# A transformer and cluster block on one core: layer norm with its roots in PSUM, an earlier start of attention, and setup loads moved beside other stages

## The chip, the cores and the metric

One core of a Trainium2 chip (trn2) runs the whole program. The metric is the device time of one execution in microseconds (us); less is better. Engines are named as in the profile: PE (TensorE, the matrix engine), DVE (VectorE), ACT (ScalarE), POOL (GpSimd) and SP (SyncE, which only issues DMAs here).

## The reference, cut to what matters

The input x has the shape 2 x 96 x 256 x 256, float32. Two layers follow each other, each added to its input.

```python
# layer 0
g   = group_norm(x, 32 groups)                 # statistics over 3 channels and all pixels
tok = overlapping 16x16 windows of g, step 14  # 19 x 19 windows per image
y   = layer_norm over the 96 channels of tok
q, k, v = y@wq, y@wk, y@wv                     # 4 heads, 16 wide for q and k, 24 for v
tok = softmax(q k^T / 4) v @ wproj + tok       # windows added up, shared strips halved
x2  = tok put back on the map
h   = gelu(layer_norm(x2) @ fc1 + b)
h   = h + gelu(depthwise_conv_5x5(h) + b)
x   = x + (h @ fc2 + b + x2)
# layer 1
x   = x + cluster(group_norm(x))               # similarity to 4 centres per region, per head
```

## The kernel before

`program` (line 2099) runs eight stages in a row. Each stage is a block: five instruction streams, one for each engine, joined by semaphores, and the next block starts when all of them have ended.

**group_norm_statistics** (line 49). SP loads x in 16 tiles of 3 MB (128 partitions x 24 KB) into a ring of four buffers, DVE takes `bn_stats` of each (line 102) and at the end one `bn_aggr` for each image (line 107). Beside it POOL and ACT lay out the taps of the convolution and store them (lines 85 and 95); ACT issues those DMAs.

**attention_setup** (line 111). POOL clears four small tables, SP issues 15 small loads of weights and constants (lines 144 to 153), and then a chain of small linked operations on DVE, PE and ACT makes the scale and shift of the group norm for each channel and image, and folds the weights of the layer norm into wq, wk and wv. The shift of q and k by the layer norm's bias is kept as a 97th row of `wqk` (lines 199 and 201).

**layer_norm** (line 217). The map is laid out as 128 partitions = four row blocks (2 images x 2 halves) of 32 channels, with three channel groups in the free dimension. There are 16 tiles of 8 rows, and each is cut into four chunks of 512 pixels: 64 chunks. 24 tiny DMAs (line 270) first copy scale and shift into this layout, and one more (line 271) loads the matrix of ones. A tile is moved by 12 DMAs of 256 KB in (line 278) and 12 out (line 286), all issued by SP, in six buffers and four tiles ahead. For each chunk ACT applies scale and shift (line 334, three instructions), PE sums over channels with the ones (line 309), DVE subtracts the mean, which it reads in PSUM (line 354), POOL squares (line 298), PE sums the squares (line 317), DVE copies the variance from PSUM to SBUF (line 358). When a tile's four variances are there, ACT makes 1/sqrt by Ln and Exp over the whole tile in SBUF (lines 339 and 341), and DVE multiplies (line 350), two tiles behind the subtraction. The order on DVE and ACT is written out by `slots`. The result goes to `y_attention` in HBM.

**attention** (line 371). The map is cut into 38 bands of 16 rows (19 per image) with 19 windows each. SP loads a band of y in two halves (`load_y`, line 496), POOL turns its eight pieces to column order (line 582), PE makes queries and keys of a piece (line 705, 512 columns) in the one bank `lin_ps`, ACT copies them to `packed` (line 655), and SP spreads a pair of pieces by eight DMAs to the heads' rows of q and k (`spread_heads`, line 522). Then each window takes one step: scores for the maximum on PE (line 720), maxima on DVE (801), turned maxima (766) added to q (842), scores (732), Exp on ACT (668), values (750), products (743), normalisation on POOL (590 to 611). At the start of the first band POOL clears two tables and q, DVE writes a row of ones into y and fills k, and PE and ACT wait for all six of these fills. All eight pieces are projected and spread before the first window's scores, which wait for all four pairs. For later bands the pieces are placed in the steps of the band before (`qk_at`).

**fc1**, **conv**, **fc2** (line 1308). fc2 works through 14 tiles; SP and ACT issue its loads and stores. Its block ends when all stores have landed (lines 1392 and 1468).

**cluster_setup** (line 1504). SP issues 18 small loads (line 1562). DVE reduces the sums that fc2 left (1624), PE gathers them once all 18 loads are there (1586), and a chain follows like that of attention_setup: among it 64 linked tiny operations (lines 1669 and 1670), then 16 for `rhs` (1675, 1676) and four copies (1679).

**cluster** (line 1682) follows and is not touched.

The order in the layer norm before is set by these lines:

```python
for k in range(AHEAD):
    load(k)
for k in range(NT):
    sp.wait_ge(z_done, (k + 1) * PER)
    ...
    if k + AHEAD < NT:
        load(k + AHEAD)
```

## Time and profile before

| | before |
|---|---|
| median of 3 runs | 6937.62 us (6933.67 to 6956.9) |
| the profiled execution: its own time | 6937.03 us |
| its span, first to last instruction | 6935.3 us |
| mean granted TensorE clock | 0.943 of full |
| PE busy | 6015.5 us (87% of the span) |
| DVE busy | 5209.9 us (75%) |
| ACT busy | 3497.3 us (50%) |
| POOL busy | 2286.0 us (33%) |
| DMA | 1252.65 MB, mean 181 GB/s |

The busy shares are means over stages with different limits. PE is at work nearly all the time in attention, whose steps the diff leaves as they are; the diff is about the stretches before 700 us and around 6050 us, where the shares of all engines are low or differ. So the reading goes by stretches and by the order of time in them, not by the table.

### The profile page before, as it was taken

The numbers are of one execution on the slowest core, as the hardware profiler recorded it, in microseconds if no ns is written. First come the engines' busy times: TensorE is split into PE (matmuls) and PEld (weight loads), VectorE is DVE, ScalarE is ACT, GpSimd is POOL, SyncE is SP. The second block draws the span as 40 slices with busy tenths as digits, with TensorE's granted clock in tenths as the row PEclk, the third lists the DMA queues.
The fourth block names the chain that finished last, engine by engine and source line by source line (L and its number), as shares of the span: only waits on it lengthen the run. The fifth ranks groups of instructions, "written<-read, shape, count | busy, mean of one in ns | idle before, by whom it ended". The sixth has DMA issues, their size and how long they took to land. (4 is left out here: it accounts for less than half of the span.)

```text
span 6935.3 us, 135783 instructions
## 1 busy us (share of the span) xinstructions
PE 6015.5 (87%) x51768; PEld 3118.6 (45%) x51768; DVE 5209.9 (75%) x7712; ACT 3497.3 (50%) x5182; POOL 2286.0 (33%) x4080
## 2 busy tenths in 40 slices
PE   0885999999999999999999689989998666578887
PEld 0332555555555555555555233335555111066663
DVE  7686888888888888888888455558887445456666
ACT  0553666666666666666666356644443111144431
POOL 0343455555554555555554656610000000000000
PEclk9997999999999999999999799999999788789987
DMA  7786344444444444444443598888987999835667
GB/s 306 192 240 179 72 106 101 101 104 106 103 108 100 103 109 102 105 101 101 107 96 71 146 269 235 237 288 345 345 341 266 283 314 316 249 90 167 189 183 248
DMA packets 761666, 1252.65 MB, mean 181 GB/s; under 512 B 159364, under 2 KB 477828, under 8 KB 730948
## 3 DMA queue, kind: packets, MB, share of 16 engines
q1 hardware_dynamic: 700532, 1090.77, 55.8%
q10 hardware_dynamic: 54560, 111.50, 5.3%
q0 software_dynamic: 5936, 41.68, 1.7%
q8 instruction: 422, 6.91, 0.4%
q14 instruction: 216, 1.77, 0.1%
HBM read 680.81 MB, written 508.40 MB: 171 GB/s over the span
## 5 line engine op out<-in xcount | busy, mean ns | idle before, releaser
L801 DVE TENSOR_REDUCE at_mz<-at_ps 128x4 bf16<-128x1024 f32 x1444 | 1772.3, 1227 | 105.3 <-PE at_ps L720 80.3
L668 ACT ACTIVATE at_E<-at_ps 128x1024 f32<-128x1024 f32 x1444 | 1399.4, 1021 | 382.6 <-PE at_ps L732 368.0
L732 PE MATMUL at_ps<-at_qaug,at_k 32*128 32x256 f32 x11552 | 830.0, 401 | 23.7 <-DVE at_qaug L842 23.7
L743 PE MATMUL at_ps<-at_E,at_vaug 128*32 128x256 f32 x11552 | 774.3, 385 | 5.5
L1282 PE MATMUL cv_ps<-cv_yin,cv_band 128*128 128x384 f32 x2304 | 745.4, 486 | 26.2 <-DMA cv_yin<-y_mlp 26.2
L1302 DVE TENSOR_TENSOR cv_yin<-cv_gl,cv_yin 64x384 f32<-64x384 f32 x1152 | 637.6, 553 | 150.3 <-ACT cv_gl L1293 142.4
L732 PEld LDWEIGHTS at_ps<-at_qaug,at_k 32*128 32x128 f32 x11552 | 523.0, 184 | 494.1 <-issue 384.5
L590 POOL TENSOR_TENSOR at_share<-at_rden,t_share 128x8 f32<-128x8 f32 x722 | 148.5, 206 | 1445.5 <-DVE at_rden L812 1445.5
L1282 PEld LDWEIGHTS cv_ps<-cv_yin,cv_band 128*128 128x128 f32 x2304 | 436.1, 189 | 335.7 <-DMA cv_yin<-y_mlp 27.1
L720 PE MATMUL at_ps<-at_k,at_q 32*128 32x256 bf16 x5776 | 574.2, 275 | 8.9 <-DMA at_k<-at_packed 7.4
L1293 ACT ACTIVATE cv_gl<-cv_ps,cv_bias 128x384 f32<-128x384 f32 x576 | 335.1, 582 | 435.8 <-PE cv_ps L1282 435.8
L842 DVE TENSOR_TENSOR at_qaug<-at_ps,at_q 128x256 f32<-128x256 f32 x722 | 306.5, 425 | 272.3 <-PE at_ps L766 272.3
L750 PEld LDWEIGHTS at_ps<-t_wv,at_y 96*128 96x128 f32 x2888 | 377.1, 190 | 297.6 <-issue 297.6
L750 PE MATMUL at_ps<-t_wv,at_y 96*128 96x96 f32 x2888 | 495.5, 294 | 0.0
L1566 POOL MEMSET cs_eps<- 96x1 f32 x1 | 0.1, 96 | 1502.8 <-POOLq L1314 1502.8
L676 ACT ACTIVATE at_xa<-at_ps,t_out_shift 96x448 f32<-96x448 f32 (+2 forms) x304 | 314.7, 1035 | 347.4 <-PE at_ps L759 347.4
L1432 DVE SCALAR_TENSOR_TENSOR f_xa<-f_ps,f_b,f_xa 128x256 f32<-128x256 f32 x384 | 226.9, 666 | 348.4 <-PE f_ps L1415 347.5
L1859 PE MATMUL cl_ps<-c_rhs,cl_xu 97*128 97x208 f32 x2048 | 448.0, 376 | 41.1 <-DMA cl_xu<-x 34.6
L1859 PEld LDWEIGHTS cl_ps<-c_rhs,cl_xu 97*128 97x128 f32 x2048 | 397.4, 211 | 111.0 <-issue 67.1
L1412 PE MATMUL f_ps<-f_sa,f_wa 128*32 128x512 f32 (+1 forms) x1728 | 237.6, 622 | 240.9 <-DMA f_sbb<-s_mlp 239.6
L743 PEld LDWEIGHTS at_ps<-at_E,at_vaug 128*32 128x32 f32 x11552 | 313.0, 109 | 287.6 <-issue 171.1
L705 PE MATMUL at_ps<-at_y,t_wqk 97*128 97x512 f32 x608 | 349.7, 658 | 55.3 <-DVE at_k L846 42.6
(217 smaller groups left out, 9596.0 us busy)
## 6 DMA issues: line engine op xcount, KB each, us to landing
cv_yin<-y_mlp SPq DMA_DIRECT2D x48, 2340.0 KB, 14.8
s_mlp<-cv_yin SPq DMA_DIRECT2D x48, 2340.0 KB, 8.4
at_rows_in<-y_attention SPq DMA_DIRECT2D x76, 768.0 KB, 6.1
gn_xin<-in_x SPq DMA_DIRECT2D x16, 3072.0 KB, 23.2
ln_xin<-in_x SPq DMA_DIRECT2D x192, 256.0 KB, 7.4
y_attention<-ln_xin SPq DMA_DIRECT2D x192, 256.0 KB, 3.8
cl_xu<-x SPq DMA_DIRECT2D x128, 384.0 KB, 3.6
at_xr<-in_x SPq DMA_DIRECT2D x68, 672.0 KB, 5.7
```

Of the source, the lines that this page charges most:

```text
L668: act.activation(E[:, m % 2, 2 * p:2 * p + 2, :], psum[:, 2 + 2 * p:4 + 2 * p, :], ACT.Exp).then_inc(exp_done, 1)
L676: act.activation(xa[:, 0:rows, cols(c)].rearrange("p r c -> p c r"), lin_ps[0:C, 0:CC * rows].rearrange("p (c r) -> p c r", r=rows), ACT.I ...
L705: pe.matmul(lin_ps, t["wqk"][:], y[:, n % 2, CK * c:CK * c + CK], start=True, stop=True).then_inc(qk_done, 1)
L720: i = pe.matmul(psum[:, g, TOK * j:TOK * j + TOK], q_upper[rows, n % 2, tokens(w, 128 * j, 128)], k_upper[rows, n % 2, tokens(w)], start=T ...
L732: i = pe.matmul(psum[:, 2 + h, TOK * j:TOK * j + TOK], k[rows, n % 2, tokens(w, 128 * j, 128)], qaug[rows, m % 2, :], start=True, stop=True)
L743: i = pe.matmul(pv_ps[32 * h:32 * h + VC, 0:TOK], vaug[:, m % 2, z, h, :], E[:, m % 2, h, z * TOK:(z + 1) * TOK], start=(z == 0), stop=(z ...
L750: i = pe.matmul(lin_ps[:, j * C:(j + 1) * C], y[0:C, n % 2, tokens(w, 128 * j, 128)], t["wv"][:], start=True, stop=True)
L801: dve.tensor_reduce(mz[:, m % 2].rearrange("p j (h c) -> p h j c", c=32)[:, 2 * p:2 * p + 2, :, DQ], psum[:, 0:2, :].rearrange("p h (j n) ...
L1282: m = pe.matmul(psum[:, n % NB, 0:3 * RUN], band[:, s, c, a, :], yin[:, s, c, 3 * u:3 * u + 3, GAP * a:GAP * a + RUN], start=(a == 0), sto ...
L1293: act.activation(gl[:, n % NG, :], psum[:, n % NB, 0:3 * RUN], ACT.Gelu, bias=bias[:, n // PARTS:n // PARTS + 1]).then_inc(gl_done, 1)
L1302: i = dve.tensor_tensor(yc, gl[half_rows(f), n % NG, :].rearrange("p (t n) -> p t n", n=RUN), yc, ALU.add)
L1859: m = pe.matmul(psum[:, 2 * half + g // 2, 256 * (g % 2):256 * (g % 2) + NFC], xu[:, n % XS, 128 * tile:128 * tile + 128], t["rhs"][:, f * ...
```

## The change

Four things are done.

1. **Statistics and setup.** The ring of the statistics has six buffers, which are those of the layer norm, and the same semaphores. The setup's weights (now 16 loads, the ones of the layer norm among them) are issued by ACT's queue during the statistics, and SP asks for the first two tiles of the layer norm behind the last tiles of the statistics. Each image's `bn_aggr` comes right behind its last tile. Scale and shift reach the layer norm's layout by three products with spread identities and two copies, not by 24 DMAs. The tables `cen_w`, `cen_shift` and `ones` go.
2. **Layer norm.** Each variance stays in its PSUM bank (a ring of six banks). ACT takes roots for two chunks at a time: Ln from PSUM to SBUF, Exp back to PSUM. DVE multiplies straight from PSUM, six chunks behind the subtraction; the copy of the variance goes. PE's variance runs two chunks behind its mean, POOL's squares have three buffers.
3. **Attention's start.** q and k are filled by DVE, band buffer 0 first. PE projects four of eight pieces up front into four banks of their own, without waiting for the fills; the other four pieces go into the first four steps. The scores of windows 0, 4, 9 and 13 wait for the pair that they need. The second half's load and the next band's are issued earlier, the residual's later. q's and k's bias leaves the 97th row and is added by ACT's copy of the products, for all 38 bands.
4. **fc2 and cluster_setup.** The 18 loads and the clears go to POOL's queue during fc2. fc2 no longer waits for its stores; cluster_setup's SP does, beside the chain. The 64 tiny operations become eight on DVE and eight copies on POOL, unlinked; `rhs` is written by two copies on POOL and two operations on DVE, and the last four copies are split between DVE and ACT.

The diff, cut to its core:

```diff
+XB, LN_AHEAD, LN_EARLY = 6, 4, 2
+LN_ROWS, GN_TILES = 8, 16
@@ group_norm_statistics
-                if m >= NBUF:
-                    sp.wait_ge(taken, m - NBUF + 1)
-                sp.dma_start(xin[:, m % NBUF, :], src[:, part * CH:(part + 1) * CH]).then_inc(loaded[m % NBUF], 16)
+                if m >= XB:
+                    sp.wait_ge(taken, m - XB + 1)
+                sp.dma_start(xin[:, m % XB, :], src[:, part * CH:(part + 1) * CH]).then_inc(loaded[m % XB], 16)
+            for k in range(LN_EARLY):
+                sp.wait_ge(taken, STEPS + k - XB + 1)
+                norm_load(sp, x, s, k)
...
+            act.wait_ge(cleared, 4)
+            for to, of in setup_weights(p, t, s):
+                act.dma_start(to, of).then_inc(s["weights_loaded"], 16)
...
+                if m % PART == PART - 1:
+                    b, n = m // PART, PART * PER
+                    dve.wait_ge(taken, m + 1)
+                    dve.bn_aggr(t["mean_var"][:, b, :], stats[:, b * n:(b + 1) * n, :]).then_inc(aggregated, 1)
@@ attention_setup
+            pool.wait_ge(s["weights_loaded"], LOADED)
+            for grp in range(CGRP):
+                pool.tensor_copy(s["spread"][:, grp, :].rearrange("p (g c) -> p g c", g=4),
+                                 t["eye"][0:C, 32 * grp:32 * grp + 32].unsqueeze(1).to_broadcast([C, 4, 32])).then_inc(spread_done, 1)
...
-            pe.matmul(ps[0:C, 3, 0:B], t["centre"][:], t["gn_shift"][:], start=True, stop=True).then_inc(pch, 1)
+            pe.wait_ge(spread_done, CGRP)
+            for grp in range(CGRP):
+                m = pe.matmul(ps[:, 3, 4 * grp:4 * grp + 2 * B], s["spread"][:, grp, :], t["gn"][:].rearrange("p a b -> p (a b)"), start=True, stop=True)
+            m.then_inc(pch, 1)
@@ layer_norm
+    PAIR, PAIRS = 2, 3
+    LAG = PAIR * PAIRS
+    SQ = 3
+    XH_AHEAD = 2
...
             def variance(n):
                 pe.wait_ge(sq_done, n + 1)
-                if n >= 2:
-                    pe.wait_ge(var_out, n - 1)
+                if n >= LAG:
+                    pe.wait_ge(z_done, n - LAG + 1)
...
+            for n in range(N + 2):
                 if n < N:
                     mean(n)
-                if n:
-                    variance(n - 1)
+                if n >= 2:
+                    variance(n - 2)
...
+            def roots(j):
+                banks = slice(root(PAIR * j), root(PAIR * j) + PAIR)
+                act.wait_ge(var_done, PAIR * (j + 1))
+                act.activation(logs[:, j % 2], psum[:, banks, :], ACT.Ln, bias=t["eps5"][:]).then_inc(log_done, 1)
+                act.wait_ge(log_done, j + 1)
+                act.activation(psum[:, banks, :], logs[:, j % 2], ACT.Exp, scale=-0.5).then_inc(rs_done, 1)
+
+            for n in range(XH_AHEAD):
+                affine(n)
+            for n in range(N + LAG):
+                if n + XH_AHEAD < N:
+                    affine(n + XH_AHEAD)
+                j = (n - LAG + PAIR) // PAIR
+                if n % PAIR == 0 and 0 <= j < N // PAIR:
+                    roots(j)
...
+            def normalised(n):
+                dve.wait_ge(rs_done, n // PAIR + 1)
+                dve.tensor_tensor(chunk(n), chunk(n), over_groups(psum[:, root(n), :]), ALU.mult).then_inc(z_done, 1)
+
+            for n in range(N + LAG):
+                if n < N:
+                    centred(n)
+                if n >= LAG:
+                    normalised(n - LAG)
@@ attention
+    FIRST = YP // 2
+        FIRST_NEEDED = [next(w for w in range(NWIN) if at(w) + PS > 2 * CC * i) for i in range(YP // 2)]
...
             nb, w = where(n)
+            if n < YP - FIRST:
+                return 0, FIRST + n
...
+        def qk_ps(n, c):
+
+            return psum[:, 2 + c, :] if n == 0 and c < FIRST else lin_ps
...
             load_y(0, 0)
+            load_y(0, 1)
+            sp.wait_ge(filled, 4)
+            spread_heads(0, 0)
+            spread_heads(0, 1)
+            load_y(1, 0)
+            spread_heads(0, 2)
+            spread_heads(0, 3)
             load_x(0, 0)
             load_x(0, 1)
-            load_y(0, 1)
-            if NB > 1:
-                load_y(1, 0)
-            sp.wait_ge(filled, 6)
-            for i in range(YP // 2):
-                spread_heads(0, i)
+            sp.wait_ge(filled_next, 2)
...
-                act.activation(packed[:, pair % 2, CK * (c % 2):CK * (c % 2) + CK], lin_ps, ACT.Copy).then_inc(qk_out, 1)
+                act.activation(packed[:, pair % 2, CK * (c % 2):CK * (c % 2) + CK], qk_ps(n, c), ACT.Identity, bias=t["qk_bias"][:]).then_inc(qk_out, 1)
...
-                    if w == 0:
+                    if n == 0 and w in FIRST_NEEDED:
+                        i = FIRST_NEEDED.index(w)
+                        pe.wait_ge(spread[i % 2], 16 * TRANSFERS * (i // 2 + 1))
+                    if n and w == 0:
...
-            dve.memset(y[C:C + 1, :, :], 1.0).then_inc(filled, 1)
-            for i in range(2):
-                dve.tensor_copy(k[:, i, :], t["one_rows"][:].to_broadcast([128, W * PS])).then_inc(filled, 1)
-            dve.wait_ge(filled, 6)
+            for i, done in enumerate((filled, filled_next)):
+                dve.memset(q[:, i, :], 0.0).then_inc(done, 1)
+                dve.tensor_copy(k[:, i, :], t["one_rows"][:].to_broadcast([128, W * PS])).then_inc(done, 1)
+            dve.wait_ge(filled, 4)
@@ fc2
-            for u in range(XA):
-                sp.wait_ge(stored[u], 16 * XLOADS * len(range(u, NTILE, XA)))
+        @block.gpsimd
+        def _(pool):
+            for to, of in setup_loads(p, t, s):
+                pool.dma_start(to, of).then_inc(s["loaded"], 16)
...
-            for u in range(XA):
-                act.wait_ge(stored[u], 16 * XLOADS * len(range(u, NTILE, XA)))
+    return [(stored[u], 16 * XLOADS * len(range(u, NTILE, XA))) for u in range(XA)]
@@ cluster_setup
         @block.sync
         def _(sp):
-            for to, of in loads:
-                sp.dma_start(to, of).then_inc(loaded, 16)
+            for arrived, count in x1_stored:
+                sp.wait_ge(arrived, count)
...
             for q in range(NREG):
-                for e in range(CH_HEADS):
-                    link(dve.tensor_scalar(ctr[:, q, e, :].rearrange("p (i j) -> p i j", j=2), quarters(cn), heads[:, e:e + 1], None, ALU.mult))
-                    link(dve.tensor_copy(xmq[:, q, e, :].rearrange("p (i j) -> p i j", j=2), quarters(xm)))
-            staged()
+                last = dve.tensor_tensor(ctr[:, q].rearrange("p e (i j) -> p e i j", j=2),
+                                         quarters(cn, q).unsqueeze(1).to_broadcast([C, CH_HEADS, 2, 2]),
+                                         heads[:].unsqueeze(2).unsqueeze(3).to_broadcast([C, CH_HEADS, 2, 2]), ALU.mult)
+            last.then_inc(stage, 1)
```

## Rows read from the trace of the kernel before

In the rows in order of time the columns are: start in us, us from the first start to the last end, engine, line, operation, out<-in, count, and in brackets the idle time of the engine before it with what released it.

**Rows 1.** In order of time, end of the statistics to the layer norm's start.

```profile
132.82 5.37 DVE L107 BATCH_NORM_AGGREGATE t_mean_var<-gn_stats 128x2 f32<-128x576 f32 x2
...
147.28 0.16 DVE L187 TENSOR_TENSOR as_m<-t_mean_var 128x2 f32<-128x2 f32 x1 [9.09 <-DMA t_one_rows<-in_k_one_rows]
...
153.10 0.23 DVE L214 TENSOR_SCALAR t_neg_eye<-t_eye 128x128 bf16<-128x128 f32 x1
...
184.96 8.56 ACT L334 ACTIVATE ln_xin<-ln_xin,ln_shift,ln_scale 128x512 f32<-128x512 f32 x12 [35.66 <-DMA ln_xin<-in_x]
```

**Rows 2.** Stretches: us, busy of five engines (instructions), PE clock, DMA share, GB/s.

```profile
169.65:222.00 52.35, 32.54 (x66) 13.74 (x66) 13.29 (x10) 18.58 (x22) 14.43 (x6) 0.97 0.99 242
...
400.00:450.00 50.00, 43.01 (x94) 17.92 (x94) 44.88 (x25) 28.11 (x32) 20.31 (x8) 0.97 0.84 240
```

**Rows 3.** In order of time, layer norm: stores of tile 4, affine of tile 8.

```profile
362.18 9.48 SPq L286 DMA_DIRECT2D y_attention<-ln_xin  x12
...
387.46 4.34 ACT L334 ACTIVATE ln_xin<-ln_xin,ln_shift,ln_scale 128x512 f32<-128x512 f32 x6 [7.09 <-DMA ln_xin<-in_x]
```

**Rows 4.** In order of time, layer norm: POOL's square beside DVE's multiply.

```profile
584.95 2.75 POOL L298 TENSOR_TENSOR ln_sq<-ln_xin 128x1536 f32<-128x1536 f32 x1 [3.36 <-DVE ln_xin L354]
585.39 3.92 DVE L350 TENSOR_TENSOR ln_xin<-ln_xin,ln_rs 128x1536 f32<-128x1536 f32 x1
```

**Rows 5.** In order of time, layer norm: the last four multiplies.

```profile
611.00 6.76 DVE L350 TENSOR_TENSOR ln_xin<-ln_xin,ln_rs 128x1536 f32<-128x1536 f32 x4 [0.29 <-ACT ln_rs L341]
```

**Rows 6.** In order of time, layer norm: two squares and a subtraction.

```profile
194.03 5.45 POOL L298 TENSOR_TENSOR ln_sq<-ln_xin 128x1536 f32<-128x1536 f32 x2 [55.06 <-DVE ln_xin L354]
...
194.76 1.75 DVE L354 TENSOR_TENSOR ln_xin<-ln_xin,ln_ps 128x1536 f32<-128x1536 f32 x1 [0.82 <-PE ln_ps L309]
```

**Rows 7.** In order of time, PE in the layer norm: first products, later ones.

```profile
187.32 7.40 PE L309 MATMUL ln_ps<-ln_xin,ln_ones 128*128 128x512 f32 x12 [36.38 <-ACT ln_xin L334]
...
564.60 2.74 PE L317 MATMUL ln_ps<-ln_sq,ln_ones 128*128 128x512 f32 x6
...
567.17 2.74 PE L309 MATMUL ln_ps<-ln_xin,ln_ones 128*128 128x512 f32 x6
```

**Rows 8.** In order of time, the first band of attention to its first scores.

```profile
633.45 0.32 SPq L496 DMA_DIRECT2D at_rows_in<-y_attention  x1
...
641.25 8.15 POOL L582 COPY at_y<-at_rows_in 96x512 f32<-96x512 f32 x4
...
647.55 2.08 PE L705 MATMUL at_ps<-at_y,t_wqk 97*128 97x512 f32 x2 [42.57 <-DVE at_k L846]
...
659.52 2.59 SPq L522 DMA_DIRECT2D at_q<-at_packed  x4
...
684.27 0.61 PE L720 MATMUL at_ps<-at_k,at_q 32*128 32x256 bf16 x4 [7.43 <-DMA at_k<-at_packed]
```

**Rows 9.** In order of time, fc2's last stores, cluster_setup, cluster's start.

```profile
6041.36 6.41 ACTq L1369 DMA_DIRECT2D x<-f_xa  x6
...
6053.00 2.85 DVE L1624 TENSOR_REDUCE cs_folded<-sums 128x48 f32<-128x1536 f32 x1 [11.75 <-PEq L1314]
...
6062.42 0.41 PE L1586 MATMUL cs_ps<-cs_folded,cs_pick 128*32 128x17 f32 x12 [28.24 <-DMA c_combine<-in_k_combine]
...
6074.67 0.23 DVE L1669 TENSOR_SCALAR cs_ctr<-cs_cn,cs_heads 96x4 f32<-96x4 f32 x1
...
6089.63 0.91 PE L1602 MATMUL cs_ps<-cs_ctr,cs_f_nat 96*97 96x64 f32 x4 [16.31 <-DVEq L1621]
...
6099.48 0.27 DVE L1984 MEMSET cl_zero<- 128x256 f32 x1 [0.63 <-PEq L1507]
```

**Rows 10.** In order of time, layer norm: a table load and Exp on ACT.

```profile
556.55 1.28 ACT L341 ACT_TABLE_LOAD   x1
...
557.84 1.91 ACT L341 ACTIVATE ln_rs<-ln_rs 128x2048 f32<-128x2048 f32 x1
```

**Rows 11.** Line 522 from 630 to 730 us, its DMAs' landing.

```profile
DMA to landing us min/median/max: 2.3/2.4/5.6
```

404 lines of the change are left out of this document (198 added, 206 removed).

## The prediction

> **What bounds the kernel now.** I read first the busy time by stretches, which shows where the limits lie, then the order of time at the four places that the diff touches.
>
> Lead-in. The statistics of the group norm end at 138.2 us [rows 1]. Their weights are only then loaded (VectorE waits 9.09 us), the small chain runs from 147.28 to 153.3, and 25 small orders (lines 270 and 271) go out before the first tile's. ScalarE takes its first tile at 184.96, having idled 35.66 us. So 47 us lie between the last statistic and the first useful work, nearly all of it queue time.
>
> Layer norm, 64 chunks in 16 tiles. One tile's whole move is 6.29 MB. The loads alone fill the DMA engines to 0.99 at 242 GB/s, the steady state moves 240 GB/s at a share of 0.84 [rows 2]: 26.2 us a tile, DMA not quite full. What paces it is a loop: stores of tile 4 begin at 362.18, and the tile loaded behind them is taken at 387.46, 25.3 us later, after ScalarE idled 7.09 us for it [rows 3]. Normalisation trails by two tiles and a part, so four tiles of lookahead leave no slack. VectorE is as close: its normalising multiply takes 3.92 us beside a square of POOL that began 0.4 us before it [rows 4], and 1.69 us (four in 6.76) once POOL is done [rows 5]: with two operands in SBUF it stands still until the square is over. The subtraction, which has one operand in PSUM, takes 1.75 us in the middle of two POOL squares (194.03 to 199.48) [rows 6]: it isn't held up. PE's three products start 2.57 us after the three before [rows 7], 5.14 us a chunk, so PE needs 20.6 us a tile.
>
> Attention's start. From 633.45 to the first scores at 684.27 are 50.8 us [rows 8]: PE's first product waits for the filled keys, and all eight chunks are projected and spread before any score.
>
> Cluster setup. VectorE's first reduction starts at 6053.00, PE's first product waits for 18 small loads until 6062.42, 64 tiny linked operations take 6074.67 to 6089.6, and the clustering starts at 6099.48 [rows 9].
>
> **The change part by part.**
>
> Lead-in. The 16 weight loads go to ScalarE's queue beside the statistics. They carry 0.44 MB, 1.8 us at the loads' 242 GB/s; of the statistics' full queue they take nothing at best and the 9.09 us of today's wait at worst, and I take 2. One aggregation (2.7 us) moves under the waits of the statistics, so these end 0.7 us earlier, near 137.5. The chain loses the 9.09 us wait, two small scalings and a copy, and gains three small products and two copies of the size of its first link, 0.16 us: 6.2 us. POOL's copies for these products wait for nothing that is late. The 24 copies by DMA go. With half a microsecond at each of two changes of stage (my estimate, between 0.3 and 1) ScalarE starts at about 144.7. Two tiles are asked for behind the last statistics; at 13 us each they land at 140 and 153, the first in time. **Gain 40 us of start.**
>
> Layer norm. The normalising multiply reads PSUM: 1.75 us like the subtraction, and the copy of the variance goes; VectorE needs 3.5 us of the 5.14. ScalarE now takes roots for two chunks at a time: six affines 4.28 (twelve took 8.56 [rows 1]), two table loads of 1.28, Ln and Exp over 1024 columns. Exp took 1.91 for 2048 [rows 10]; half of that, 0.96, is the lower bound, its whole the upper. I take 1.1 each, near the half: 9.0 us a pair beside PE's 10.3. Writing the roots to PSUM isn't in the trace and has the same bounds; with both at 1.91 ScalarE needs 10.7 a pair, still under the DMA's pace below. POOL's square, 2.7 us, is covered, and so is its wait for a freed buffer, now of three. Each variance keeps its bank until its roots are used; with six banks PE's variance waits for the multiply six chunks before, a loop of 30.8 us for work of about 20. Lag falls to six chunks. The last store becomes possible after chunk 4k+9 is centred, and the load behind it is needed for chunk 4k+16: seven chunks of 5.14, less 2.57 for the product, 3.5 for VectorE and 2.2 for the affine, 27.7 us against the 25.3 needed. So the loop lets go, barely. Next is DMA: 240 GB/s at 0.84 is 286 GB/s at a full share, hence 22.0 us a tile, against PE's 20.6. SP issues the same 24 orders a tile in the same sequence, behind the same wait for the normalised tile.
>
> Timeline: PE begins at 147 with its clock low (twelve products took 7.40 us [rows 7]) and is at its pace by 155.4. Tile 0 is normalised at 197.6, tile 4 lands at 223 (PE wants it at 227). Eleven tiles more at 22.0 bring tile 15 at 465, 13 us after PE would want it, and after another 36 us (four chunks, the last variance, roots, two multiplies) the last normalisation ends at 501. Before, the last multiply ended at 617.8, and 15.7 us later the next stage began [rows 5, 8]; I keep the 15.7, since the last twelve stores are the same. End at 517, against 633.4. **Gain, with the 40: 117 us**; paced by PE it would be 132, with DMA at 23 a tile 106.
>
> Attention's start. POOL could turn the first half of the band 7.8 us after the stage began, and four turns took 8.15 us while VectorE filled keys [rows 8]; its fill now still overlaps them, so the first two are ready at 11 (between 8, and the 14.1 at which the first product ran). VectorE's own fill, now of q too, is over at some 14 and late for nobody. Pair 0 takes two products of 2.08 with a copy behind, 5 us; eight spreading orders of 0.65 [rows 8], 5.2 us; 2.4 us to land [rows 11]. First scores at 23 to 24, not 50.8. Against this the four other chunks go into steps 0 to 3: four products of 2.08 us at the cold clock, up to 8 us; their copies are covered by waits. The second half's load is now ordered before the residual loads. Scores of windows 4, 9 and 13 wait for their own pair, which lands before 50 by the same prices. **Gain 21**, between 12 and 28. Bias by ScalarE's copy replaces a copy of the same size: 0 in the sum; bounds are nothing and a small operation's 0.2 us for each of 304 copies; it would reach the end only where ScalarE sets a step. The row of ones leaves PE's time as it is.
>
> Cluster setup. The stores' landing no longer holds the stage: the last order is out at 6047.8, so the start is 4.9 us earlier. The wait for loads goes: 9.4 from start to product becomes 3.1, gain 6.3. The 64 operations in 14.9 us become 8 on VectorE (copies go to POOL beside them), at 0.23 us (14.9 over 64) to 0.5, 2 in all: gain 13. After the products 20 linked copies become four with two on ScalarE: gain 5 of the 9.85 that end the stage. That is 29. The 18 loads, 0.46 MB, move to POOL's queue in a stage where DMA is busy: 1.9 us by 242 GB/s, bounds 0 and 9.4. **Gain 27.**
>
> Sum: 117 + 21 + 27 = 165. The profiled execution took 6937.0 (span 6935.3 and 1.7 around it), the median 6937.6. Forecast **6772**.
>
> **The rivals.**
>
> Loop stays (0.09): the slack of 2.4 us is eaten by landing times that grow with a fuller queue, and tiles keep 26.2 us. Tile 15 then lands at 511, and the stage ends at 563, 46 us late on my sum: 6818. For it: the present loop binds just so [rows 3]. Against: lag falls by over a tile.
>
> ScalarE becomes the bound (0.06): with a settling time behind each table load of a size with the load itself, a pair needs 4.28 + 2 times 2.6 + 2.2 = 11.7, 5.9 a chunk, 32 pairs 376 us: 30 us above my stage, 6802. Against: the load starts at 556.55, takes 1.28, and Exp starts at 557.84, so nothing lies between [rows 10]. The Trainium skill, ScalarE: Activation LUTs, section What ACT_TABLE_LOAD costs, states a drain of about 1.38 us beside the load's 1.28; by that rule the time would be this rival's. The trace does not agree.
>
> The PSUM operand doesn't spare the multiply (0.04), the change not doing what it says: 1.75 and 4.4 us a chunk on VectorE, 24.8 a tile, 45 us more: 6815. Against: the subtraction that POOL's squares left alone [rows 6].
>
> Slower (0.02): PE's clock stays at 1.2 GHz, half of full, through the layer norm, as at its start, where twelve records took 7.40 us and six later ones start 2.57 apart [rows 7]. Then 10.3 us a chunk, 658 us in all; the stage ends near 830, 196 later than now: with 48 of gains elsewhere 7085. It decides from some 33 of 64 chunks at that clock. Against: the steady stretch was granted 0.97 of full [rows 2], and PE will have fewer pauses. The same at about half of the chunks would leave the time unchanged (0.01).
>
> **How the numbers follow.** My forecast has 0.78, and its own range is 6745 to 6800: 132 + 28 + 30 at best, 106 + 12 + 22 at worst. The range of 6742 to 6812 adds the ScalarE rival and leaves the loop and the multiply out. Over 0.3% (21 us, about what can be told from no change) faster: all but these two, 0.97; within it 0.01; slower 0.02.
>
> **What would show it.** ScalarE's first affine near 145; multiplies of 1.75 us beside POOL's squares; DMA share over 0.95 at 280 GB/s from 230 on; a period of 22 us between first stores; the next stage at 517; first scores 23 us behind it; 29 us less between the last sum of fc2 and the clustering. A period of 26, Ln waiting for a busy ScalarE, or low clock after 155 would prove me wrong.

## The result, and the profile after

The changed kernel takes 6739.12 us (median of 4 runs, 6728.26 to 6745.97), the kernel before 6941.45 beside it (4 runs, 6933.67 to 6956.9): a ratio of 0.9707, 95% interval 0.969 to 0.9723, 202 us faster. The forecast was 6772, range 6742 to 6812: the right direction, but the gain was 37 us larger than forecast and the time 3 us below the range. The two profiled executions, 6937.03 and 6728.26, are 208.8 apart, and so are their spans. Cut at fixed places of the program, the two traces give:

| stretch | before | after | gain | forecast |
|---|---|---|---|---|
| start of the program to start of attention | 633.45 | 503.70 | 129.75 | 117 |
| start of attention to first scores | 50.82 | 26.08 | 24.7 | 21, both rows together |
| first to last scores | 3137.9 | 3141.5 | -3.6 | |
| last scores to fc2's first product | 1589.1 | 1585.4 | 3.7 | 0 |
| fc2's first product to its last | 621.2 | 598.7 | 22.5 | 0 |
| fc2's last product to the first of clustering | 71.9 | 42.2 | 29.7 | 27 |
| the clustering's first product to the end | 830.9 | 828.9 | 2.0 | 0 |

Two rows carry the miss: the layer norm with 12.8 us, and fc2's products, which the change doesn't touch, with 22.5.

**Layer norm.** First the lead-in, in order of time (columns as in the rows before the prediction):

```profile
134.99 2.75 DVE L119 BATCH_NORM_AGGREGATE t_mean_var<-gn_stats 128x2 f32<-128x576 f32 x1
...
139.48 0.27 DVE L180 TENSOR_TENSOR n_m<-t_mean_var 128x2 f32<-128x2 f32 x1 [1.74 <-PEq L59]
...
145.29 0.23 DVE L208 TENSOR_SCALAR t_neg_eye<-t_eye 128x128 bf16<-128x128 f32 x1
146.02 14.21 ACT L315 ACTIVATE n_xin<-n_xin,n_affine 128x512 f32<-128x512 f32 x20 [4.39 <-PEq L125]
148.30 11.01 PE L291 MATMUL ln_ps<-n_xin,n_group_ones 128*128 128x512 f32 x18 [4.38 <-ACT n_xin L315]
```

VectorE's 9.09 us wait for weights and the 35.66 us of ScalarE [rows 1] are gone. Then a stretch of the steady state (columns: stretch, its length, busy time and instructions of PE, PEld, DVE, ACT and POOL, granted clock, DMA share, GB/s), followed by the waits between 150 and 470 us:

```profile
400.00:450.00 50.00, 50.00 (x118) 22.12 (x117) 32.79 (x20) 43.09 (x48) 25.96 (x11) 1.00 1.00 298
```

```profile
DVE n_xin L341 <- PE ln_ps L291: 121.1, 63, 8.3
...
ACT n_xin L315 <- DMA n_xin<-in_x: 36.7, 12, 9.2
ACT ln_logs L321 <- PE ln_ps L299: 10.0, 5, 4.8
...
PEld ln_ps L291 <- ACT n_xin L315: 2.2, 4, 0.7
```

TensorE is busy in all of the 50 us, with 118 records where [rows 2] had 94. ScalarE waits 36.7 us in all for tiles, yet the products wait 2.2: its two chunks of lead absorb it. The stores show the period; these are tiles 1, 2 and 11:

```profile
219.44 8.84 SPq L267 DMA_DIRECT2D y_attention<-n_xin  x12
...
240.04 8.05 SPq L267 DMA_DIRECT2D y_attention<-n_xin  x12
...
425.67 8.31 SPq L267 DMA_DIRECT2D y_attention<-n_xin  x12
```

(425.67 - 219.44) / 10 = 20.6 us a tile: TensorE's pace, with the DMA engines at 6.29 MB / 20.6 = 305 GB/s. The multiply beside POOL's square, which took 3.92 us [rows 4], and the roots:

```profile
225.28 1.28 ACT L321 ACT_TABLE_LOAD   x1
226.57 1.11 ACT L321 ACTIVATE ln_logs<-ln_ps,t_eps 128x1024 f32<-128x1024 f32 x1
227.70 1.28 ACT L323 ACT_TABLE_LOAD   x1
...
229.00 1.03 ACT L323 ACTIVATE ln_ps<-ln_logs 128x1024 f32<-128x1024 f32 x1
...
341.35 1.75 DVE L345 TENSOR_TENSOR n_xin<-n_xin,ln_ps 128x1536 f32<-128x1536 f32 x1
341.51 2.75 POOL L282 TENSOR_TENSOR ln_sq<-n_xin 128x1536 f32<-128x1536 f32 x1 [2.48 <-DVE n_xin L341]
```

**Attention's start**, in order of time; POOL turns four pieces in 10.01 us, not 8.15 [rows 8], and the scores start 26.1 us behind the stage:

```profile
509.53 10.01 POOL L575 COPY at_y<-at_rows_in 96x512 f32<-96x512 f32 x4 [4.83 <-DMA at_rows_in<-y_attention]
...
511.19 2.07 PE L698 MATMUL at_ps<-at_y,t_wqk 96*128 96x512 f32 x2 [29.79 <-POOL at_y L575]
...
517.61 5.49 PE L698 MATMUL at_ps<-at_y,t_wqk 96*128 96x512 f32 x6 [4.34 <-POOL at_y L575]
...
520.48 2.52 SPq L514 DMA_DIRECT2D at_q<-at_packed  x4
...
529.78 0.61 PE L716 MATMUL at_ps<-at_k,at_q 32*128 32x256 bf16 x4 [6.69 <-DMA at_k<-at_packed]
```

**Cluster setup**, in order of time, to be read against [rows 9]:

```profile
5864.30 6.39 ACTq L1400 DMA_DIRECT2D x<-f_xa  x6
5871.17 2.84 DVE L1693 TENSOR_REDUCE cs_folded<-sums 128x48 f32<-128x1536 f32 x1 [6.98 <-PEq L1345]
...
5874.31 0.41 PE L1654 MATMUL cs_ps<-cs_folded,cs_pick 128*32 128x17 f32 x12 [17.19 <-DVE cs_folded L1695]
...
5887.23 0.77 DVE L1733 TENSOR_TENSOR cs_ctr<-cs_cn,cs_heads 96x16 f32<-96x16 f32 x8
...
5892.74 0.27 DVE L2049 MEMSET cl_zero<- 128x256 f32 x1 [0.63 <-PEq L1577]
```

From fc2's last order to the clustering's first operation: 22.0 us instead of 51.7.

**fc2**, the transfers in 547 us of its steady stretch, first of the kernel before, then of the changed one:

```profile
DMA packets 86347, 171.00 MB, mean 313 GB/s; under 512 B 7682, under 2 KB 8450, under 8 KB 86317
```

```profile
DMA packets 89765, 177.52 MB, mean 325 GB/s; under 512 B 7966, under 2 KB 8734, under 8 KB 89732
```

The same queues carry the same lines, 4% faster. fc2 waits mostly for its transfers (TensorE idles 239.6 us for them before, 219.0 after), so this shortens it.

### The profile page after: what moved, and what is told of

It is laid out like the page before. It is cut to its first block and busy times, and to the rows that moved or that the text cites. A ratio compares the mean times of both kernels' runs of the same rounds, so it can differ in the third digit from the quotient of the medians.

```text
span 6726.5 us, 135701 instructions
## 1 busy us (share of the span) xinstructions
PE 5966.7 (89%) x51772; PEld 3104.2 (46%) x51772; DVE 5047.8 (75%) x7576; ACT 3571.6 (53%) x5248; POOL 2288.5 (34%) x4109
## 5 line engine op out<-in xcount | busy, mean ns | idle before, releaser
L1313 PEld LDWEIGHTS cv_ps<-cv_yin,cv_band 128*128 128x128 f32 x2304 | 436.4, 189 | 336.7 <-DMA cv_yin<-y_mlp 27.8
L1471 DVE SCALAR_TENSOR_TENSOR f_xa<-cs_ps,f_b,f_xa 128x256 f32<-128x256 f32 x384 | 227.1, 668 | 328.1 <-PE cs_ps L1454 327.3
L1451 PE MATMUL cs_ps<-f_sa,f_wa 128*32 128x512 f32 (+1 forms) x1728 | 237.5, 622 | 220.4 <-DMA f_sbb<-s_mlp 219.0
L648 ACT ACTIVATE at_packed<-at_ps,t_qk_bias 128x512 f32<-128x512 f32 x304 | 208.8, 687 | 413.1 <-PE at_ps L698 413.1
L1489 ACT ACTIVATE f_squared<-f_xa 128x1280 f32<-128x1280 f32 (+1 forms) x84 | 99.1, 1180 | 560.0 <-issue 450.4
```

The source lines that it names most:

```text
L1313: m = pe.matmul(psum[:, n % NB, 0:3 * RUN], band[:, s, c, a, :], yin[:, s, c, 3 * u:3 * u + 3, GAP * a:GAP * a + RUN], start=(a == 0), sto ...
```

## The experiments

Sixteen kernels ran. "fc2's products" is the time from the start of its first product with `sa` to the start of the last.

**Each part alone.** e1 is the kernel before with the fourth part, e2 with the third, e3 with the first two, e6 with the lead-in alone. The functions are taken over whole, and `program` calls them; for e6 the layer norm's loop of before works on the new buffers:

```diff
 def program(...):
-        fc2(...); cluster_setup(nc, p, tab, t)                            # e1
+        x1_stored = fc2(..., t, s, inner); cluster_setup(..., s, x1_stored)
-        attention(...)                                                    # e2: before's body and 97th row
+        attention(...)                                                    # the changed body and t["qk_bias"]
-        group_norm_statistics(...); attention_setup(...); layer_norm(...) # e3
+        s = norm_tables(nc, inner); group_norm_statistics(..., s); attention_setup(..., s); layer_norm(..., s)
 def layer_norm(...):                     # e6
-    xin = sb("xin", ...); ones = sb("ones", ...)
+    xin, ones = s["xin"], s["group_ones"]
-    sp.dma_start(scale / shift ...)  x24
+    scale, shift = s["affine"][:, 0, :], s["affine"][:, 1, :]
     # slots(), the variance copy and the roots of a whole tile stay
```

> The kernel before with the fourth part alone (fc2 does not wait for its stores, the setup's 18 loads on POOL's queue, the folded small operations). The forecast had 27 us for this part. The trace of the changed kernel reads differently: from fc2's last product to the first product of the cluster stage it is 41.1 us instead of 70.8 (29.7 less), and the stretch from fc2's first product to its last is 599.8 us instead of 622.3 (22.5 less), with the same products and the same transfers at 325 instead of 313 GB/s. Theory F (fc2's faster transfers belong to this part: the addresses of its tables, or what it does on POOL's queue): 50 to 56 us faster, 0.992 to 0.993, and fc2's products span about 600 us. Theory V (fc2's transfers vary from execution to execution or with what runs before them, the part gives only its own 30): 28 to 32 us faster, about 0.9955, and fc2's products may span anything from 600 to 625 us.

> The kernel before with the third part alone (the fills on DVE, four pieces projected first, FIRST_NEEDED, the bias in ScalarE's copy). The trace of the changed kernel says 24.8 us to the first scores and 3.6 us given back until the last: 21 us faster, 0.997, if that is the part's. The forecast was 21 (12 to 28). Rival: the gain up to 44 us that is missing between the forecast and the result sits after the attention (fc1 5 us shorter between its first and last products), because the bias copy leaves something changed; then 26 us or more. fc2 is here the code of before: theory F expects its products to span 620 to 624 us, theory V anything from 600 to 625.

> The kernel before with the first two parts (lead-in and layer norm). The trace of the changed kernel puts the start of the attention 129.75 us earlier. If nothing of what comes later is touched: 128 to 132 us faster, 0.981 to 0.9815. The attention starts at 503 to 505 us. The forecast was 117 with the layer norm paced by its transfers; here it is paced by TensorE at 20.6 us for a tile. fc2's products: theory F expects 620 to 624 us, theory V 600 to 625.

> The kernel before with the lead-in alone: the first part, with the layer norm's loop, its variance copy, its roots for a whole tile and its two products of lag as before. The forecast's working had 40 us for the earlier start, if the loop keeps its 26.2 us for a tile. Theory 1: attention starts at 590 to 596 us instead of 633.5, and the run is 38 to 43 us faster (0.994). Theory 2 (TensorE's clock and the loop's queues are helped by the earlier start, or the loop was held by late loads): 50 us or more. What is left of e3's 128.5 is the loop's.

| kernel | median us | ratio to before (95%) | gain of medians | fc2's products |
|---|---|---|---|---|
| e1, cluster setup | 6895.94 | 0.9934 (0.9913 to 0.9955) | 44 | 614.4 |
| e2, attention | 6915.26 | 0.9964 (0.9951 to 0.9978) | 25 | 621.5 |
| e3, lead-in and layer norm | 6811.62 | 0.9815 (0.9793 to 0.9838) | 129 | 623.2 |
| e6, lead-in | 6899.21 | 0.9947 (0.9932 to 0.9962) | 43 | 625.4 |

The three gains add up to 198 of the 202. Each carries an interval of some 9 to 16 us either way, so an interaction of the parts is not seen, but one of 10 us could hide. e3's attention starts at 504.6, e6's at 595.1 against 633.45 before, so the lead-in is worth 38 us of start and the loop the other 90. In e6's loop the multiplies keep their old form and the period stays at 26 us, although the first tiles are early: what holds that loop is not how it starts. e1 lies between its two theories: its setup takes the expected 29.5 us less, fc2's products 6.8 less in the profile, and the medians say 44. Theory V gave 28 to 32, theory F 50 to 56; the interval (31 to 60) leaves both.

**What fc2 gains, and from what.** The changed fc2 has the same loop; but the setup's tables now lie in SBUF ahead of its own tiles. e5 runs the fc2 stage of before six times in one program (stages of the clustering left out), in turns 1, 3 and 5 behind tables of the setup's sizes:

```diff
-        fc2(nc, p, xs, sdr, x1, tab)
-        cluster_setup(nc, p, tab, t)
-        cluster(nc, x1, out, t, slot_loaded, slot_stored, slot_counts)
+        for turn in range(6):
+            with ExitStack() as inner:
+                pads = setup_tables(nc, inner, False) if turn % 2 == 0 else None
+                fc2_turn(nc, p, xs, sdr, x1, tab, sems, base)
+        # out <- x1
```

> The kernel before with its fc2 stage run six times over, one after the other, in place of once (same inputs, same outputs). Turns 1, 3 and 5 have the setup's tables laid out in SBUF ahead of fc2's own, so that fc2's tiles lie at the addresses of the changed kernel; turns 2, 4 and 6 have the addresses of the kernel before. Everything else in the six is the same code. The cluster stages are left out, the output is a copy of x1; so the time is about 6,935 less 880 plus 5 times 680 and the copy. In the traces so far fc2's products span 621.2, 621.5 and 623.2 us with the code and addresses of before, and 598.7, 614.4 and 619.0 with those of the change. Theory F1 (the addresses make the transfers faster): turns 1, 3 and 5 are each shorter than each of 2, 4 and 6, by 5 us or more. Theory V (it varies): the two kinds overlap. Theory F2 (something else of the changed code, such as how it starts behind the loads on POOL's queue): all six stay at 620 to 624.

The products span 609.0, 612.6, 607.2, 628.6, 609.0 and 628.2 us. Stretches from each turn's middle:

```profile
5453.00:6000.00 547.00, 376.63 (x2952) 59.16 (x2951) 287.13 (x399) 92.46 (x146) 0.00 (x0) 0.84 1.05 318
6130.00:6680.00 550.00, 377.29 (x2948) 59.18 (x2944) 286.32 (x398) 91.79 (x145) 0.00 (x0) 0.84 1.04 314
6810.00:7360.00 550.00, 379.35 (x2987) 59.81 (x2984) 289.70 (x404) 91.74 (x144) 0.00 (x0) 0.84 1.04 319
7486.00:8036.00 550.00, 366.72 (x2904) 58.02 (x2896) 280.09 (x392) 87.67 (x138) 0.00 (x0) 0.83 1.05 308
8181.00:8731.00 550.00, 376.80 (x2976) 59.60 (x2968) 288.49 (x402) 93.10 (x146) 0.00 (x0) 0.84 1.05 319
8858.00:9408.00 550.00, 368.96 (x2899) 58.07 (x2896) 279.92 (x392) 89.07 (x141) 0.00 (x0) 0.83 1.05 308
```

The DMA share (next to last column) is full in all six; the last column is not the same: 318, 319, 319 against 314, 308, 308 GB/s. Each turn at the new addresses is shorter than each at the old ones, though turn 2 by less than the 5 us asked for. F2 falls, and the addresses (theory F1) are the likely cause; three turns against three, always in the same alternation, need other orders beside them.

Which address? e9, e13 and e14 put pads between the tiles:

```diff
+        if pads[0]: sb("pad", [128, pads[0] // 4])
         sa = sb("sa", [128, 2, 2, PHASES, LINE])
+        if pads[1]: sb("pad", [128, pads[1] // 4])
         sbb = sb("sbb", [128, 2, PHASES, LINE])
+        if pads[2]: sb("pad", [128, pads[2] // 4])
         xa = sb("xa", [128, XA, CGRP, TILE_BLKS, 2, W])
```

> As the six turns of fc2 before, cluster stages left out again, with pads between fc2's tiles. The tiles begin at these offsets within 512 bytes (the sums' and squares' tile sa, its second half sbb, the residual tile xa): turn 1: 128, 256, 64 (the kernel before); turn 2: 128, 256, 0; turn 3: 64, 192, 64; turn 4: 128, 256, 256; turn 5: 0, 0, 0; turn 6: 64, 192, 0 (the changed kernel). xa is moved in 2,048-byte lines both ways, and each of its lines starts at the same offset as the tile. Theory X (it is xa's 512-byte alignment): turns 2, 5 and 6 take 674 to 682 us from one start to the next, or 606 to 612 for the products, turns 1, 3 and 4 take 680 to 697, 612 to 628. Theory S (it is where sa and sbb lie): turns 3 and 6 are short, 1, 2 and 4 long. Theory N (neither, it is the distance between the tiles or mere scatter): no such order.

> The same six layouts of fc2's tiles as in e9 in another order: offsets within 512 bytes of sa, sbb, xa: turn 1: 0, 0, 0; turn 2: 128, 256, 256; turn 3: 64, 192, 64; turn 4: 128, 256, 64 (before); turn 5: 128, 256, 0; turn 6: 128, 256, 256. In e9 their products spanned 628, 602, 621, 630, 615 and again 602. If the layout decides, these values come back within some 6 us and in this order, whatever the turn; if the place in the sequence or chance decides, they don't.

> A third order: turn 1: 64, 192, 64; turn 2: 0, 0, 0; turn 3: 128, 256, 64 (before); turn 4: 128, 256, 256; turn 5: 64, 192, 0 (the changed kernel); turn 6: 128, 256, 0. By e9: 621, 628, 630, 602, 615, 615. If the layout decides, 128, 256, 256 is the shortest again, 10 us or more under the kernel before's; if not, the order changes.

| bytes past a multiple of 512: sa, sbb, xa | fc2's products in e9, e13, e14 (e5) |
|---|---|
| 128, 256, 64 (before) | 631.0, 627.5, 642.4 (612.6, 628.6, 628.2) |
| 64, 192, 64 | 621.9, 624.4, 615.7 |
| 64, 192, 0 (changed) | 615.8, 605.3 (609.0, 607.2, 609.0) |
| 128, 256, 0 | 615.6, 610.1, 615.0 |
| 128, 256, 256 | 602.6, 599.0, 601.5, 619.5 |
| 0, 0, 0 | 628.8, 603.0, 605.1 |

(The layout with xa at 256 had two turns in e13. The expectations were written with turns read half a microsecond shorter.) Nine turns with xa at 64 take 625.8 us in the mean, fifteen with xa at 0 or 256 take 609.8. Single turns scatter: 628.8 and 619.5 lie on the wrong side, 612.6 and 615.7 too, and e9's values came back within 6 us only for 128, 256, 0; its order alone would have misled (0, 0, 0 looked slow). None of e9's three theories came out of e9 alone, and its theory X fell in the form it had, an alignment of 512 bytes: xa at 256 gave the shortest turns. What holds over 24 turns is xa's offset. With xa at 64, moving sa and sbb from 128, 256 to 64, 192 made it about 8 us shorter (628.4 to 620.7), which these runs don't settle.

The traces also record each DMA packet's size and time, and in fc2 the packets of 2,048 bytes are xa's alone. From 30 us behind the first product to 30 us ahead of the last, their mean time is 90.9 to 94.6 ns in each of the 14 stages with xa at 64 (nine turns and five whole programs), and 86.8 to 90.2 ns in each of the 24 with xa at 0 or 256 (fifteen and nine): the two kinds don't overlap. The means are 92.3 and 88.1 ns; 4.2 ns on fc2's 49,152 such packets (50.3 MB in, as much out) over 16 engines is an estimate of 13 us, most of the 16. The slow turn at 0, 0, 0 has its xa packets at 90.2 ns; what was slow in it are the 2,592-byte packets of sa and sbb, 165.0 ns where its repeats show 153.8 and 153.3, so that part is scatter.

xa is moved in lines of 2,048 bytes. The Trainium skill, DMA: Bandwidth & Descriptors, section How a descriptor splits into AXI transactions, says by the vendor's account that a transaction must start at a multiple of 256 bytes, so that the first one of a line starting elsewhere begins at the multiple below it, and the bytes ahead of the line still cost beats. My estimate by that rule is nine transactions for eight and 66 beats for 64 for a line at 64, so 3% more beats on xa's lines; these are half of the stage's bytes (41,856 packets of 2,048 in the 171 MB above), which makes 1.6% of the stage. The mean difference here is more, 2.6% of the stage (16.0 of 625.8) and 4.8% of xa's packet time, so the beats alone don't give its size; the rule does name the offsets that came out short (0 and 256). No run tried 128 for xa, so the 256 itself isn't shown.

Then in the whole kernel, both ways, by a pad of one line:

```diff
+        sb("pad", [128, 192 // 4])    # e15, kernel before: xa from 64 to 256
+        sb("pad", [128, 64 // 4])     # e16, changed kernel: xa from 0 to 64
         xa = sb("xa", [128, XA, CGRP, TILE_BLKS, 2, W])
```

> The kernel before with nothing but a pad of 192 bytes ahead of fc2's xa, which so begins at 256 within 512 bytes, and its 2,048-byte lines at a multiple of 128. Over the four kernels of six turns, the 15 turns with xa at a multiple of 128 spanned 609 us in the mean (598 to 628), the 9 turns with xa at 64 spanned 625 (612 to 642). Theory X (the alignment of xa alone): fc2's products 600 to 612 us, the run 14 to 20 us faster, 0.9975. Rival (the turns were something of their own, in the whole kernel it is the shift of sa and sbb): 620 to 625, no faster.

> The changed kernel with a pad of 64 bytes ahead of fc2's xa, which so begins at 64 within 512 bytes, as in the kernel before; all else stays, the 18 loads on POOL's queue and the missing wait among it. Theory X: fc2's products 618 to 628 us, the run 13 to 18 us slower than the changed kernel: 6751 to 6758, 0.973. Rival (it is where sa and sbb lie, or the part's other edits): 6736 to 6744, 599 to 612 us.

e15: 6930.19 against 6949.18, ratio 0.997 (0.9957 to 0.9984), so 19 us (11 to 30) for a pad that does no work. fc2's products (the first columns after the count are the duration of one in ns, then first and last start):

```profile
L1413 PE MATMUL f_ps<-f_sa,f_wa x1728: 389/622/1063, 5412.2 to 6016.3; 128*32 128x512 f32 x152, 128*32 128x256 f32 x40
```

604.1 us. e16: 6750.26 us, ratio 0.9723 (0.9707 to 0.974), 11 us above the changed kernel's median; the direction is theory X's, but the profiled 614.7 us lies under its 618, and the interval overlaps the changed kernel's (0.969 to 0.9723), so e16's time by itself doesn't show the loss. Its packets do: xa's take 91.6 ns, in the changed kernel 87.9; in e15 they take 87.8, in the kernel before 91.3. Over the profiles of whole programs, five with xa at 64 span 614.7 to 625.4, mean 621.2, and nine with xa at 0 or 256 span 598.7 to 619.0, mean 607.3: 14 us. The 22.5 of the two profiles compared above are this and some luck of the changed kernel's execution: its 598.7 is the shortest of the nine.

**What the DMA engines can give in the layer norm.** e4 takes engine work away from the changed kernel, so that its output is no longer the layer norm, and leaves the transfers; e10 and e11 are e4 with the buffers at offsets 0 and 384 instead of 64:

```diff
-                pool.tensor_tensor(sq[:, n % SQ], chunk(n), chunk(n), ALU.mult)
+                pool.tensor_tensor(sq[:, n % SQ, 0:1], chunk(n, slice(0, 1)), chunk(n, slice(0, 1)), ALU.mult)
-                for grp in range(CGRP):            # variance: three products
+                # one product, group 0
-                for grp in range(CGRP):            # affine
+                for grp in range(CGRP - 1):
```

> The changed kernel with less work for the engines in the layer norm and the same transfers: squares and variance sum only channel group 0 (2 of 3 groups left out), and the affine map leaves group 2 as it is. TensorE then wants 8 of 12 products for a chunk (13.7 us for a tile), ScalarE about 14.5. The tile period is what the DMA engines give at most with this order of transfers. The forecast's step: 286 GB/s, 22.0 us for a tile of 6.29 MB. That step already fell, since the changed kernel runs at 20.6 (305 GB/s). Theory 1 (the engines were at their limit, and 0.97 to 1.01 of share is all): 20.0 to 20.6 us stays. Theory 2 (the share reads full but there is more to be had, as in the convolution's 375 GB/s): 17 to 19 us.

> The thinned layer norm of e4 with its six input buffers moved from byte offset 64 to 0 within 512 (loads and stores of 8,192-byte lines). e4 took 20.5 us for a tile with TensorE idle for the transfers a fifth of the time. Theory X (512-byte alignment makes SBUF transfers faster, as it seems to in fc2): 19.5 us or less for a tile. Rival (long lines do not care): 20.3 to 20.6.

> The same with the buffers at offset 384, where the kernel before has them. The forecast took its ceiling of 286 GB/s from that kernel (240 at a share of 0.84). Theory A (the ceiling itself depends on the offset, and moved when the change moved the buffers from 384 to 64): 21.5 to 22 us for a tile. Theory B (the share of busy time is no linear scale, the ceiling was 305 all along): 20.3 to 20.6.

Now the transfers rule; of e4:

```profile
250.00:300.00 50.00, 35.98 (x75) 14.19 (x74) 34.06 (x20) 39.16 (x42) 10.39 (x10) 0.95 1.01 330
```

```profile
225.58 8.44 SPq L267 DMA_DIRECT2D y_attention<-n_xin  x12
...
427.16 8.33 SPq L267 DMA_DIRECT2D y_attention<-n_xin  x12
```

TensorE is busy 36 of 50 us, and ten tiles take 201.6 us: 20.2 a tile, 312 GB/s. The same ten take 195.8 (19.6, 321 GB/s) at offset 0 and 198.7 (19.9, 317 GB/s) at 384, where the kernel before has its buffers. So the ceiling is 312 to 321 GB/s, also at the offset that the kernel before had. e11's 19.9 lies below both its theories (20.3 to 20.6, and 21.5 to 22) and far from A; e10's 19.6 lies between its two. 286 was not the ceiling at any of the three offsets. The order 64, 384, 0 is within what one profile each can tell. e4's theory 1 was right, its expectation for the rival (17 to 19) fell: the loop sits within 5% of both its limits. Even with a third of the products gone, the whole kernel takes 6717 to 6732 us.

**The multiply and PSUM.** e7 lets Exp write to SBUF, so the multiply has both operands there.

```diff
+        roots_sb = sb("roots", [128, LAG, CW])
-                act.activation(psum[:, banks, :], logs[:, j % 2], ACT.Exp, scale=-0.5)
+                act.activation(roots_sb[:, ...PAIR], logs[:, j % 2], ACT.Exp, scale=-0.5)
-                dve.tensor_tensor(chunk(n), chunk(n), over_groups(psum[:, root(n), :]), ALU.mult)
+                dve.tensor_tensor(chunk(n), chunk(n), over_groups(roots_sb[:, root(n) - 2, :]), ALU.mult)
```

> The changed kernel, but the roots go to SBUF (a ring of six chunks) and the normalising multiply reads both operands from SBUF; everything else stays, the variance in PSUM too. Theory 1 of the forecast (a multiply with an operand in PSUM does not hold up the POOL squares and is not held up, two SBUF operands are): the multiply takes over 1.75 us, or POOL's square over 2.75, in the stretch where both work, but both have slack, since TensorE and the transfers pace the loop: a tile stays at 20.6 us, 6730 to 6745. Rival (the PSUM operand is what the change lives from): DVE or POOL become late for TensorE, a tile takes 22 us or more, 20 us slower or more. Rival 3: SBUF costs nothing at all, the multiply even gets faster.

```profile
299.62 1.75 DVE L346 TENSOR_TENSOR n_xin<-n_xin,ln_roots 128x1536 f32<-128x1536 f32 x1
299.78 4.19 POOL L283 TENSOR_TENSOR ln_sq<-n_xin 128x1536 f32<-128x1536 f32 x1 [0.96 <-DVE n_xin L342]
```

6750.46 us, ratio 0.9724 (0.9711 to 0.9736), attention's first scores 1.4 us later. The multiply keeps its 1.75 us, since here it starts first, and now POOL's square stands still until it is over: 4.19 us instead of 2.75. That holds for all 58 squares that start during a multiply; the 58 that do so in the changed kernel take 2.75. In [rows 4] the square started first and the multiply paid. POOL has room for 4.19 in 5.14, so the period stays at 20.6 (theory 1). The time is 11 us above the changed kernel's and 5 above theory 1's 6745, with intervals that overlap; of the 15.5 us between the two profiled executions 8.7 lie in fc2's products (607.4), so the layer norm isn't shown to be slower. What PSUM's operand saves is thus real but not what paces the loop in the new order.

**The bias.** e8 returns it to the product as its 97th row.

```diff
-                act.activation(packed[...], qk_ps(n, c), ACT.Identity, bias=t["qk_bias"][:])
+                act.activation(packed[...], qk_ps(n, c), ACT.Copy)
-        y = sb("y", [C, 2, W * PS])
+        y = sb("y", [C + 1, 2, W * PS])    # row C set to one by VectorE, waited for by TensorE
```

> The changed kernel with the queries' and keys' bias back in the product as its 97th row, and ScalarE's copy without bias (304 of them, 687 ns with bias in the changed kernel, 597 before); the row of ones is set by DVE ahead of its fills. From its first scores to its last the attention takes 3136 to 3138 us with the row and 3141 with the changed kernel. Theory 1 (the bias in the copy costs a little on the path): 3136 to 3138 here, ScalarE's copy back at 0.60 us. Theory 2 (the four products in steps 0 to 3 cost it): 3141 here as well. The first scores come 0 to 2 us later, for the row of ones.

6742.07 us, 0.9713 (0.9699 to 0.9727), as the changed kernel. ScalarE's copy falls back from 687 to 597 ns (the function changed with the bias column, from Identity to Copy), and the attention still takes 3142.8 us from first to last scores: theory 2. The four products in the first steps cost it. Here are the first 100 us behind the first scores, of the kernel before and of the changed one:

```profile
684.30:784.30 100.00, 95.26 (x1024) 51.39 (x1025) 75.41 (x111) 55.76 (x76) 32.65 (x82) 0.90 0.21 38
```

```profile
529.80:629.80 100.00, 96.65 (x994) 50.34 (x994) 72.81 (x108) 56.69 (x77) 34.77 (x85) 0.91 0.39 72
```

30 records of TensorE fewer, at 1099 in the next 100 us of either kernel: 2.7 us behind, most of the 3.6.

**A faster version?** e12 begins the large tiles of the layer norm, attention, fc1 and the clustering at a multiple of 512 bytes; fc2's stay where the changed kernel has them, with xa at 0.

```diff
+    "pad": ([128, 112], F32)    # attention_tables: layer norm and attention, 64 -> 0
+    sb("pad", [128, 104])       # fc1 before x, 96 -> 0
+    sb("pad", [128, 40])        # cluster before xu, 352 -> 0
```

> The changed kernel with three pads (448, 416 and 160 bytes), so that the layer norm's buffers and the attention's tiles, fc1's input tile and the cluster stage's tiles begin at a multiple of 512 bytes (64, 96 and 352 before); fc2's xa is there already. Theory X: fc1's products span 630 to 640 us instead of 641 to 647 (it is near its transfers' limit only in stretches), the layer norm stays at TensorE's 20.6, the cluster stage waits less for cl_xu; in all 5 to 15 us faster than the changed kernel, 0.969 to 0.9695. Rival: nothing, 0.9705 to 0.9715.

6737.37 us, 0.9713 (0.97 to 0.9727): nothing, its rival's figure. fc1's products span 643.1 us (641.4 to 650.1 in the others). In these stages the offset doesn't show; that only stretches of them are bound by transfers is my reading of it, not tested. No version beats the changed kernel.

## Why the prediction was wrong by its size and right by its mechanisms

- **Lead-in**: right. Predicted ScalarE's first affine at 144.7, it came at 146.02; 40 us of start, 38 in e6's trace, 43 in its medians.
- **Layer norm's loop**: mechanism right, the failed step is "Next is DMA: 240 GB/s at 0.84 is 286 GB/s at a full share, hence 22.0 us a tile". The share of busy time was taken as a scale of the rate. It isn't: the same transfers reach 305 in the changed kernel and 312 to 321 when nothing else binds. So the tiles went at TensorE's 20.6, and the text's own alternative, 132 for a loop paced by PE, was the case: 129.75 measured, 12.8 above the 117 in the sum. (By its own terms that alternative is 130, not 132: the text lets tile 15 come 13 us after PE would want it.) The loads' stretch in [rows 2], 0.99 of share at 242 GB/s, should have warned: it gives 244 at a full share, so a full share has no one rate.
- **ScalarE**: right. Ln 1.11 and Exp 1.03 us against 1.1; the rival of a settling time behind the table load is refuted: loads of 1.28 us at 225.28 and 227.70, and Ln and Exp at 226.57 and 229.00. The Trainium skill, ScalarE: Activation LUTs, section What ACT_TABLE_LOAD costs, gives about 1.28 us for the load and a drain of about 1.38 us with it: the first agrees with this trace, the drain isn't in it.
- **The multiply at 1.75 us**: right in size. But in the new order it starts 0.16 us ahead of the square, and e7's starts first too and takes 1.75 us with both operands in SBUF; what the PSUM operand spares here is the square's wait, 2.75 us against 4.19.
- **PE's clock low throughout**: refuted, the granted clock is 1.00 in every stretch of 50 us from 150 to 450, with 113 to 118 records of TensorE in each.
- **Attention**: 24.7 to the first scores (forecast 26.8 to 27.8 before the products in the steps), 3.6 given back: 21.1 against 21. POOL's turning, 10.01 us for 8.15, is one of the reasons for the first figure. e2's medians say 25. The bias costs nothing, as taken.
- **Cluster setup**: 29.7 against 29 less 2 for the loads in a busy stage; those 2 did not show.
- **fc2**: the step that was missing altogether. The working asked what of the change runs in fc2 (18 loads) and not where it puts fc2's tiles. In the sum it stood at nothing. It is worth 14 us by the whole programs' profiles, 19 by e15, and 22.5 in the two profiles compared.
- **The range**: 12.8 and 14 more than the sum give 6745, inside the range's edge; the rest, to the measured 6739, is fc2's scatter and other small things. The range ran from a best case of the same terms to a worse one and a rival's time; a term outside the list had no room. Its ends are also 2 or 3 us off their own terms: 132 + 28 + 30 from 6937 is 6747, not 6745, and 106 + 12 + 22 is 6797, not 6800. In the same way the multiply rival's 45 us on 6772 are 6817, not 6815.

The remaining 5.7 us between the two profiles, mostly fc1's products (646.4 and 641.4), I read as scatter: over thirteen profiles of whole programs with the same fc1 they span 641 to 650.

## What to carry to other kernels

A stage's ceiling for transfers is read from a stretch where they alone bind, with the same mix of loads and stores, or bounded by the fastest stretch of like lines; scaling a rate by the busy share understated it by a tenth here. When a change allocates anything ahead of another stage's tiles, that stage's addresses move: in a stage bound by transfers of 2 KB lines, look at the tile's offset first, because a pad gave 19 us here and its reverse took some 11. And ask of each conflict between two engines who pays for it: moved to an engine with slack, it did not lengthen the tile's period here.

## What was not expected of the hardware

- 2,048-byte lines at 64 bytes past a multiple of 256 in SBUF, read and written: 2.6% more time for the stage than at 0 or 256 (625.8 and 609.8 us), at the same full DMA share, and 92.3 against 88.1 ns for one such packet.
- A square of POOL that starts 0.16 us behind a multiply with two SBUF operands takes 4.19 us instead of 2.75; with [rows 4], where the multiply was the later one, whichever of the two starts second waits. With one operand of the multiply in PSUM neither did.
- ScalarE's copy of 128x512 from PSUM takes 90 ns more as Identity with a bias column than as Copy without one (687 and 597 ns, 304 of each).
- Ln and Exp in turn bring a table load of 1283 ns before each (32 loads in the layer norm before, 64 after), and the next operation starts 0.01 us behind it where it waits for nothing else.
